# Three feed-forward stages: the turn of a finished chunk's normalized rows stands two or three blocks further on in the next chunk

## What is computed

```python
x = x + 0.5 * _L0_ffn_ref(_layernorm(x), ...)     # stage F0a
x = x + _L0_attn_ref(_layernorm(x), ...)          # stage A0
x = x + 0.5 * _L0_ffn_ref(_layernorm(x), ...)     # stage F0b
x = x + 0.5 * _L1_ffn_ref(_layernorm(x), ...)     # stage F1a
x = x + _L1_attn_ref(_layernorm(x), ...)          # stage A1
x = x + 0.5 * _L1_ffn_ref(_layernorm(x), ...)     # stage F1b

# _L0_ffn: 2 shared experts and 8 routed ones, each 256 wide
silu(x @ w1.T) * (x @ w3.T) @ w2.T                # times the token's weight for a routed expert
# _L1_ffn: 8 experts, each 512 wide
square(relu(x @ c_fc)) @ c_proj                   # for the 2 best experts of a token, with a capacity
```

## Time and profile before

| | before |
|---|---|
| median of 3 runs | 3040.31 us (3038.96 to 3042.32) |
| the profiled execution: its own time | 3041.84 us |
| the profiled execution: its span, first to last instruction | 3040.1 us |
| TensorE busy | 2598.1 us, 85% |
| VectorE busy | 2307.1 us, 76% |
| ScalarE busy | 2223.2 us, 73% |
| GpSimd busy | 1637.9 us, 54% |
| mean granted clock of TensorE | 0.864 |

### The profile page before, as it was taken

How to read it: one execution, slowest core, us unless ns; L and a number is a source line. 1 busy time by engine, 2 the same in 40 slices (tenths; PEclk the granted TensorE clock), 3 DMA queues, 4 the chain that set the end, 5 groups by cost and what they waited for, 6 DMA issues and landing times. The chain is left out here.

```text
span 3040.1 us, 42347 instructions
## 1 busy us (share of the span) xinstructions
PE 2598.1 (85%) x12208; PEld 1727.1 (57%) x12208; DVE 2307.1 (76%) x4329; ACT 2223.2 (73%) x2497; POOL 1637.9 (54%) x1288
## 2 busy tenths in 40 slices
PE   7999979999799996999975878778687777589998
PEld 6877756666587774878852323223232232268887
DVE  7677756777566777898977788787787877498887
ACT  5555536656455555777849999999999999777776
POOL 4667642122266763545536676776756667334444
PEclk9999979999899997999976667766666767689999
DMA  3111111111111112111100000000000000021111
GB/s 134 42 56 41 41 23 41 44 43 43 51 42 56 41 41 96 45 43 45 51 0 1 1 1 1 0 1 1 1 1 1 1 1 1 22 92 56 42 55 42
DMA packets 24917, 101.62 MB, mean 33 GB/s; under 512 B 5856, under 2 KB 7904, under 8 KB 15680
## 3 DMA queue, kind: packets, MB, share of 16 engines
q1 hardware_dynamic: 23360, 99.51, 9.5%
q10 hardware_dynamic: 1408, 0.34, 0.0%
HBM read 82.33 MB, written 2.62 MB: 28 GB/s over the span
## 5 line engine op out<-in xcount | busy, mean ns | idle before, releaser
L1911 POOL TENSOR_TENSOR A_Y<-A_Y,A_U 128x2048 f32<-128x2048 f32 x86 | 390.0, 4558 | 222.1 <-ACT A_U L1958 222.1
L1994 DVE TENSOR_SCALAR A_U<-ps 128x1024 f32<-128x1024 f32 x256 | 309.0, 1217 | 127.0 <-POOL A_Y L1911 58.1
L2000 DVE SCALAR_TENSOR_TENSOR A_U<-ps,A_U 128x1024 f32<-128x1024 f32 x256 | 310.8, 1214 | 57.3 <-PE ps L2144 57.3
L2144 PE MATMUL ps<-A_QT,A_KT 9*128 9x512 f32 x512 | 180.8, 702 | 193.6 <-DVE A_U L2000 162.0
L477 POOL TENSOR_TENSOR F0b_h<-F0b_h,dn 128x512 f32<-128x512 f32 x128 | 212.0, 1661 | 111.9 <-DVE F0b_h L409 111.8
L477 POOL TENSOR_TENSOR F0a_h<-F0a_h,dn 128x512 f32<-128x512 f32 x128 | 212.1, 1662 | 104.6 <-DVE F0a_h L409 104.5
L2144 PEld LDWEIGHTS ps<-A_QT,A_KT 9*128 9x128 f32 x512 | 65.7, 252 | 329.6 <-DVE A_U L2000 237.4
L1911 POOL TENSOR_TENSOR dn<-dn,A_U 128x2048 f32<-128x2048 f32 x42 | 190.3, 4551 | 112.8 <-ACT A_U L1958 112.8
L1958 ACT ACTIVATE A_U<-A_U 128x2048 f32<-128x2048 f32 (+1 forms) x96 | 236.5, 2464 | 0.0
L2116 PE MATMUL ps<-A_Y,A_VA 128*32 128x512 f32 x688 | 228.9, 799 | 5.8 <-DVE A_OT L1893 3.0
L1350 DVE CUSTOM_DVE_ANT_0 ps<-ps,A_mask 128x256 f32<-128x256 f32 (+1 forms) x512 | 184.8, 421 | 58.6 <-PE ps L1430 57.8
(11 more groups left out here) (417 smaller groups left out, 8134.7 us busy)
## 6 DMA issues: line engine op xcount, KB each, us to landing
dn<-weight_rows SPq DMA_DIRECT2D x32, 1024.0 KB, 4.6
F1a_cwb<-weight_rows SPq DMA_DIRECT2D x16, 1024.0 KB, 4.6
F1b_cwb<-weight_rows SPq DMA_DIRECT2D x16, 1024.0 KB, 4.6
A_KZ<-A_KT SPq DMA_DIRECT2D x132, 48.0 KB
A_QZ<-A_qs SPq DMA_DIRECT2D x96, 64.0 KB, 2.0
dn<-in_down SPq DMA_DIRECT2D x2, 2048.0 KB, 12.2
stage<-in_up SPq DMA_DIRECT2D x1, 2560.0 KB, 13.8
X<-in_x SPq DMA_DIRECT2D x4, 512.0 KB, 7.0
```

The source lines that it names most:

```text
L1911: eng.tensor_tensor(flat(y_slot(m, h)), flat(y_slot(m, h)), flat(Um[:, h % UR]), ALU.add).then_inc(s["t_ready"], 1)
L1994: eng.tensor_scalar(u_step(n), d_pair(n), 0.0, None, ALU.max).then_inc(s["dp_vector"], 1)
L2000: eng.scalar_tensor_tensor(out=u, in0=g_pair(), scalar=CLAMP, in1=u, op0=ALU.min, op1=ALU.mult).then_inc(s["u_ready"], 1)
L2144: last = eng.matmul(ps[:, 4 + b, :], KT[r:r + 9, pair, kt * P:(kt + 1) * P], QT[r:r + 9, pair, :], start=True, stop=True)
```

## The change

In the table AT, three numbers of each row grow: turn, copy and score by 2 for the gated stages (first row) and by 3 for the squared ones (second row).

```diff
-        AT = ({"y_copy": 4, "turn_back": 6, "add": 7, "root": 8, "apply": 9, "turn": 11, "copy": 12, "score": 14},
-              {"y_copy": 5, "turn_back": 8, "add": 9, "root": 11, "apply": 13, "turn": 16, "copy": 18, "score": 20})
+        AT = ({"y_copy": 4, "turn_back": 6, "add": 7, "root": 8, "apply": 9, "turn": 13, "copy": 14, "score": 16},
+              {"y_copy": 5, "turn_back": 8, "add": 9, "root": 11, "apply": 13, "turn": 19, "copy": 21, "score": 23})
```

## The result

| | before | after |
|---|---|---|
| median (12 runs each) | 3042.04 us | 3048.51 us (3046.68 to 3051.45) |
| ratio | | 1.0025, 95% interval 1.0017 to 1.0032 |
| span of the profiled execution | 3040.1 us | 3049.5 us |

The changed kernel is slower by 6.5 us by the medians, 5.2 to 9.7 by the interval. The forecast was +7.9. It was counted from a median of 3040.31 over 3 runs, where 12 runs now give 3042.04; so that the forecast time (3048.2) and the measured one (3048.51) lie 0.3 apart is partly luck, and the difference, 7.9 against 6.5, is the fair comparison.

What follows compares the result with a forecast made beforehand. TensorE was taken to set the chunk time. The moved waits gain 0, the turn adds 6.2 us in gated stages and 1.7 in F1a: +7.9 on a median of 3040.31, 3048.2 us, range 3044.5 to 3053.0.

Steps and rivals of the forecast that it cites:

- The wait: In F0a, F0b and F1a, the turn's wait moves to up(12) or down(12), still held by VectorE: gain 0.
- The turn in the open, gated stages: F0a and F0b: the turn's four transposes, unhidden at their later place, add 0.44 us a chunk, 14 chunks, +6.2 us.
- F1a: +0.24 forecast: F1a: the later turn adds 0.44 us, less 0.20 of a small wait at down(15); 7 chunks, +1.7 us.
- Rival 1: Up(12) and down(12) not held by VectorE, so the waits go: faster, about 3016 us; chance 0.06.
- the price: Gated chunks if up(12) is not held: 1.78 us lost, 0.44 paid for the turn, 1.34 us less a chunk.
- Rival 2: F1a saves its 3.9 us wait while gated stages lose 6.2: about 3042.6 us; within-0.2% cases together have chance 0.13.
- Rival 3: Longer gated waits lower TensorE's granted clock behind them: 25 us more, 3073 us; chance 0.03.
- 9 x 0.2: Cost per gated wait if a block of nine matmuls ran at the low clock, each 0.2 us slower.
- The row of 4.87 us busy in 10: Stretch 388 to 398: TensorE busy only 4.87 of 10 us, granted clock still 1.00; used against the clock falling.
- No other engine comes near: Reading of busy times in F0a, F1a and F1b chunks: TensorE is busy nearly throughout and sets the chunk time.

Runs made afterwards that it cites:

- e1: Kernel before with only the gated stages' turn, copy and score two blocks later (13, 14, 16), F1a's row unchanged: ratio 1.0020, 3047.1 us.
- e3: Kernel before with only the gated stages' turn, copy and score one block later (12, 13, 15): ratio 1.0019, 3047.9 us.
- e12: Kernel before with root after block 7 in both rows, and gated apply at 10, turn 12, copies 13, scores 15: ratio 0.9916, 3016.8 us.
- e2: Kernel before with only F1a's turn, copy and score three blocks later (19, 21, 23): 3047.7 us, one run.
- e5: Kernel before with only the normalization (apply) one block later, at 10 and 14, turn left at 11 and 16: ratio 1.0089, 3070.8 us.
- e4: Changed kernel with the normalization (apply) one block later, at 10 gated and 14 in F1a: ratio 0.9972, 3035.1 us.
- e11: Changed kernel with apply one block later (10 and 14) and GpSimd weighing only 64 of 512 columns: 3020.0 us, one run.

## Why the prediction was right

**The wait: 0 gained.** Held to the hundredth: 1.90 us before up(12) now as then, and 0.06 us from the low part's end to down(12) in F1a. It was read from what stood second in TensorE's queue and third in VectorE's.

**The turn in the open, gated stages: +0.44 forecast, +0.47 and 0.48 measured**, in 14 chunks. From the first turn-back to the last, F0a is 299.23 us against 295.94 and F0b 305.82 against 302.48: +3.3 each, 6.6 in all for the 6.2 forecast. The rows show the turn at 0.35 + 0.31 - 0.23 = 0.43. Laid over each other start by start (medians of six chunks of F0a), the two kernels differ by 0.01 us up to the turn, by 0.45 at the second matmul behind it, and by 0.47 five matmuls further on. So some 0.02 a chunk come just behind the turn, in matmuls that the forecast took at the bare beat; what makes them is open. e1 and e3 show the same 0.47, so it is no chance of one run.

**F1a: +0.24 forecast, +0.24 to 0.25 measured** in the chunks inside the stage. The whole stage grew by 1.4 (313.64 against 312.22) and not by 1.7, because its last chunk ends in a wait for GpSimd's split (L503), which took most of the last 0.24. I had left the stage's end out.

**The sum.** 3.3 + 3.3 + 1.4 = 8.0 us in the three stages, for 7.9 forecast. The medians differ by 6.5. The profiled span grew by 9.4, of which A0 and A1, which the change doesn't touch, make 0.45 (-1.55 and +2.0) and the stretch to F0a's first turn-back 0.85; such stretches wander from one execution to the next. They are also why 6.5 and 8.0 are no contradiction.

**Rival 1** needed the multiply of block 10 to be done when TensorE got to up(12). This change didn't meet its condition. In e12 apply at 10 lets that multiply go first, and the turn fills the short wait for block 11's. Its gated chunks are 1.31 and 1.30 us below the kernel before, for the 1.34 of the price. That its time is the one that rival 1 named (3016.8 for 3016) is partly luck: F1a gave 1.05 a chunk in place of 0.75, and the kernel before ran at 3041.7 beside it. **Rival 2** fell with e2. **Rival 3** didn't come: in the 10 us round the new wait TensorE is busy 8.34 and the granted clock 1.00.

```profile
149.00:159.00 10.00, 8.34 (x36) 6.24 (x35) 8.94 (x17) 4.58 (x8) 7.42 (x5) 1.00 0.00 1
```

But e5 showed the mechanism as real, behind a wait of 2.33 us. The 1.6 us that a fall cost there are close to rival 3's 9 x 0.2 = 1.8. The row of 4.87 us busy in 10 had made me think it farther off than it is, and I had stopped reading too early: the granted clock was 1.00 up to 398, and low from 398.1 on, after TensorE had stood idle from 394.9. The stretch behind it, in the kernel before:

```profile
398.00:408.00 10.00, 2.50 (x9) 2.02 (x10) 2.32 (x13) 3.26 (x6) 4.14 (x2) 0.51 0.00 0
```

So the row that decided against rival 3 didn't show that the clock stays up behind such a stretch. The Trainium skill ("TensorE: Matmul & The Clock Gate", on a second failure mode of the clock gate) says that short idles between groups of matmuls, where they are frequent, make the clock swing. One wait of 1.5 us a chunk did not do it (0 of 14 chunks), and one of 2.33 did (8 of 14).

**Two loose readings of rows 1** cost nothing. "No other engine comes near" holds in F0a (VectorE 31.05 of 43.51), but in F1a VectorE is busy 41.30 of 45.53. And the rows show three single chunks, not four; F0b's is given above.

## What to carry over

When one engine waits for a thing, look at who is next in its queue and what that one waits for: if the next instruction waits for the same chain, the first wait is a place where work is free, and moving the work away makes it dear. Fill a forced wait with the pieces that can go anywhere, and shorten the wait at its source. Here the source was the root on GpSimd, two numbers in the same table, which gave 20 us where moving the turn alone lost 6.5.

## What the runs showed of the hardware

VectorE's four `xn` operations (128x128, float32) took 1.12 us with GpSimd's operations cut short, 2.07 in the kernel before and 3.08 in e4. The view of L141 by itself in F0a gives the single ones, shortest, median and longest in ns; in this order, the kernel before, e4, and e11.

```profile
L141 DVE TENSOR_SCALAR xn<-X,mv,rstd x28: 333/334/1303, 108.4 to 371.2; 128x128 f32 x24, 128x128 f32<-128x128 f32 x4
```

```profile
L141 DVE TENSOR_SCALAR xn<-X,mv,rstd x28: 332/826/1337, 108.9 to 371.7; 128x128 f32 x24, 128x128 f32<-128x128 f32 x4
```

```profile
L141 DVE TENSOR_SCALAR xn<-X,mv,rstd x32: 334/336/347, 109.4 to 389.9; 128x128 f32 x24, 128x128 f32<-128x128 f32 x8
```

In the kernel before, the first of each four took 1.30 us and the other three 0.334. The first began at 151.87, just behind the start of GpSimd's weighing (L477 at 151.81, 1.28 us long), and ended at 153.17, 0.08 after the weighing. In e4 two weighings ran one behind the other, and two of each four took 1.32 to 1.34, each ending 0.09 after one of the weighings. That is exclusion until the other operation ends, not a slower pace. The Trainium skill ("SBUF — State Buffer", on who interferes with whom) says that VectorE and GpSimd share one pair of ports as a lock, which `tensor_scalar` can take, and that the later one blocks until the other's instruction ends; these rows agree, with the 0.08 to 0.09 us from the weighing's end to `xn`'s.

A TensorE matmul of 512 columns that had been waited for started 0.05 to 0.06 us after the end of the operation that released it, and the next one followed 0.34 us later in place of 0.227 (up(10) in the kernel before, up(12) in the changed one).

Inside the gated chunks the granted clock fell to the low level (1.2 GHz) in 8 of 14 at a wait of 2.33 us (e5), and in none of 14 at waits of 1.5 us (the changed kernel).
